# A cross-network tower on one core: a third PSUM buffer for VectorE's groups, and the turned rows in the gram product's buffer

## The chip, the cores and the metric

The kernel runs on one core of one Trainium2 chip. The metric is the device time of one execution in microseconds (us). Engines are TensorE (PE, with its weight loads shown as PEld), VectorE (DVE), ScalarE (ACT), GpSimd (POOL) and SyncE (SP, which issues DMAs).

## The reference

512 samples look up 39 rows of 16 numbers. Three cross layers follow, each of them all products of the samples' features with the layer's input, multiplied by a filter; then a small multilayer network:

```
e = stack([tbl_f[ids[:, f]] for f in range(39)], axis=1)      # 512 x 39 x 16
x0 = xk = e
for W in (f0, f1, f2):
    z = einsum('bfd,bgd->bfgd', x0, xk).reshape(b, f * g, d)
    cur = einsum('bpd,pm->bmd', z, W)                         # b x 128 x 16
    outs.append(cur); xk = cur
z = sum(concatenate(outs, axis=1), axis=-1)                   # 512 x 384
h = relu(concatenate([z, dense_ctx], axis=1) @ W_top1 + b_top1)
h = relu(h @ W_top2 + b_top2)
y = h @ W_top3
```

All of it is float32.

## The kernel before

The batch is cut into 16 blocks of 32 samples (512 columns of sample and depth), a block into 4 tiles of 128 columns. For layer 1 a tile's columns are the stationary operand: TensorE multiplies them by the whole filter in 10 **groups** of up to 512 outputs, which are 4 of the 39 features each. Written (t, g) below is group g of tile t. Each group is three matmuls, of high and low parts (lines 752, 753, 756), into one PSUM buffer of 512 float32, a whole bank. `PATTERN` gives groups 0, 2, 3, 5, 7, 8 of a tile to ScalarE ("a", three buffers psa in a ring) and groups 1, 4, 6, 9 to VectorE ("d", two buffers psd in a ring). ScalarE scales each 128 outputs by a feature value (`x0c`, line 607) into `parts`; VectorE adds its scaled groups onto what ScalarE has left there (line 503), so the n-th d group of a tile waits for the n-th a group too. When all ten are in, VectorE reduces them to `cur1` (line 485, `finish_tile`). `parts` and `cur1` exist twice, for even and odd tiles.

TensorE may start a group when its buffer is free: `act_prods` counts ScalarE's finished groups, `acc_steps` VectorE's. In between, at fixed places of its stream, TensorE does the next block's layer 0 (`layer0`, 7 steps k of pair products; k = 0, 1, 6 as plain float32 at line 713, the others as three split matmuls), turns the next block's feature rows so that they are per-partition scalars (`turn_x0`, line 721, after (1, 5), into `pst`), and after the last group of a tile makes the gram product of the tile before (`grams`, line 730, into `psg`, two passes of 320 columns). ScalarE copies the turned rows to `x0c` (`scalars`), the grams to `gram` (`gram_out`), layer 0's result to `x1h` (`high_part`) and the high parts of pair products to `z0h` (`pair_high_part`).

GpSimd makes the pair products (`z0`, line 341) and low parts `z0l` (line 348), spreads `x0c` for the gram product (`spread`, line 357), and fetches embeddings three blocks ahead, one index column and gather per feature quartet (`row_numbers`, line 329, and `gather`). `row_numbers` for column c waits until VectorE has done 6 + c of the block's 16 d groups. All queues are in program order; the order is written by hand in tables such as `ZH_AT` and `SCALARS_AT`. Blocks 1 to 13 are one hardware loop on TensorE, VectorE and ScalarE, and blocks 1 to 12 on GpSimd; gathers end with block 12.

After block 15 comes layer 2, by the grams (39 steps of three matmuls), and the network on top, whose first layer takes `ps0`, `pst`, `psa0`, `psa1` as its buffers.

Of the kernel before, what the change touches and what calls it, by code (L numbers as in the profile page):

```python
# [25 lines left out]
F32 = mybir.dt.float32  # L26
# [3 lines left out]
ACT = mybir.ActivationFunctionType  # L30
AX = mybir.AxisListType

B, F, D = 512, 39, 16
M = 128
BB = 32
NBLK = B // BB
COLS = BB * D
TILES = 4
TB = BB // TILES
# [3 lines left out]
ROWS = SPT * F  # L43
# [4 lines left out]
FX = F + 1  # L48


PATTERN = ["adaadadaad", "adaadadaad", "adaadadaad", "adaadadaad"]
D_RING, A_RING = 2, 3
D_OFF = [sum(p.count("d") for p in PATTERN[:t]) for t in range(TILES + 1)]
A_OFF = [sum(p.count("a") for p in PATTERN[:t]) for t in range(TILES + 1)]
ND, NA = D_OFF[TILES], A_OFF[TILES]
SLOTS = max(p.count("a") for p in PATTERN)
assert ND % D_RING == 0 and NA % A_RING == 0
assert all(p.count("a") == SLOTS and p.count("d") <= SLOTS for p in PATTERN)


# [15 lines left out]
HIGH_AT_FIRST = {(3, 2): 0, (3, 3): 1, (3, 5): 2}  # L76
LOW_AT = {(2, 2): 0, (2, 3): 1, (3, 0): 2}
LOW_AT_FIRST = {(3, 1): 0, (3, 2): 1, (3, 3): 2}
SCALARS_AT = {(2, 3): 0, (2, 5): 1, (3, 2): 2}
PIECES = [(0, 2), (2, 4), (4, L0T)]  # L80
FIRST_PIECES = [(0, 1), (1, 3), (3, 5), (5, L0T)]
GATHERS_FROM = 6
# [21 lines left out]
def starts(b):  # L104

    return isinstance(b, int) and b == 0


def build(nc, tables, ids, w0a, w0b, w1, w2, wt1, bt1, wt2, bt2, wt3, dense, mask, ident, out):
    scratch = nc.dram_tensor("x0_rows", (F + SHIFTS, BB, D), F32, kind="Internal").ap()  # L110
    scr_rows = scratch.rearrange("f b d -> f (b d)")
    H1T, H2T = wt1.shape[1] // 128, wt2.shape[1] // 128

    with ExitStack() as ctx:
# [70 lines left out]
                return w2early[:, M * a:M * b]  # L185
            return w2late[:, M * (a - W2_EARLY):M * (b - W2_EARLY)]

        psd = [ctx.enter_context(nc.psum_tensor(f"psd{i}", [128, 512], F32)) for i in range(D_RING)]
        psa = [ctx.enter_context(nc.psum_tensor(f"psa{i}", [128, 512], F32)) for i in range(A_RING)]
        ps0 = ctx.enter_context(nc.psum_tensor("ps0", [128, 512], F32))  # L190
        pst = ctx.enter_context(nc.psum_tensor("pst", [128, 512], F32))
        psg = ctx.enter_context(nc.psum_tensor("psg", [128, 512], F32))

        ids_in, w0_in, w1_in, const_in, mlp_in, wt2_in, w2a_in, w2b_in = (
            sem(n) for n in ("ids_in", "w0_in", "w1_in", "const_in", "mlp_in", "wt2_in", "w2a_in", "w2b_in"))
# [22 lines left out]
        y_d = sem("y_d")  # L218
# [237 lines left out]
        def _(dve):  # L456
# [32 lines left out]
            def block_of(b, ahead, at=None):  # L489
                for t in range(TILES):  # L490
                    T = b * TILES + t
                    groups = [g for g in range(NG) if PATTERN[t][g] == "d"]
                    for n, g in enumerate(groups):
                        d = D_OFF[t] + n
                        y = psd[d % D_RING]
                        if n == 0:
                            dve.wait_ge(x0c_ready, T + 1)

                        dve.wait_ge(act_prods, b * NA + A_OFF[t] + n + 1)
                        dve.wait_ge(y_d, b * ND + d + 1)  # L500
                        for j in range(min(GF, F - GF * g)):
                            acc = lanes(parts[:, t % 2, n, :], j)
                            op = dve.scalar_tensor_tensor(acc, y[:, M * j:M * j + M],  # L503
                                                          x0c[:, t, GF * g + j:GF * g + j + 1], acc,
                                                          ALU.mult, ALU.add)
                        op.then_inc(acc_steps, 1)
                        if (t, n) == (0, 0):
                            low_part(b, TILES - 1)
                        if ahead:
                            if (t, n) == (SUM_AT_FIRST if starts(b) else SUM_AT):  # L510
                                sum_cur0(b + 1, at)
                            low_at = LOW_AT_FIRST if starts(b) else LOW_AT
                            if (t, n) in low_at:
                                low_part(b + 1, low_at[t, n])
                    finish_tile(b, t)
# [41 lines left out]
        def _(act):  # L557
# [23 lines left out]
            def scalars(b, t):  # L581
                act.wait_ge(tr_done, b + 1)
                if not starts(b):
                    act.wait_ge(acc_steps, (b - 1) * ND + D_OFF[t + 1])
                    act.wait_ge(x0d_ready, (b - 1) * TILES + t + 1)
                act.activation(x0c[:, t, 0:F], pst[:, ROWS * t:ROWS * t + F], ACT.Copy).then_inc(x0c_ready, 1)

            def gram_out(T, at):
                act.wait_ge(g2_done, T + 1)
# [3 lines left out]
            def block_of(b, ahead):  # L593
                for t in range(TILES):
                    T = b * TILES + t
                    groups = [g for g in range(NG) if PATTERN[t][g] == "a"]
                    for n, g in enumerate(groups):
                        a = A_OFF[t] + n
                        y = psa[a % A_RING]
                        act.wait_ge(y_a, b * NA + a + 1)  # L600
                        if n == 0:
                            act.wait_ge(x0c_ready, T + 1)
                            if t >= 2 or not starts(b):
                                act.wait_ge(c1_ready, T - 1)
                        dst = parts[:, t % 2, n, :]
                        for j in range(GF):
                            op = act.activation(lanes(dst, j), y[:, M * j:M * j + M], ACT.Copy,  # L607
                                                scale=x0c[:, t, GF * g + j:GF * g + j + 1])
                        op.then_inc(act_prods, 1)
                        if n == 1 and (t >= 2 or not starts(b)):  # L610
                            at = (slice((T - 2) * TB, (T - 1) * TB) if isinstance(T, int)
                                  else bass.ds((T - 2) * TB, TB))
                            gram_out(T - 2, at)
                        zh_at = ZH_AT_FIRST if starts(b) else ZH_AT
                        if ahead and (t, n) in zh_at:
                            pair_high_part(b + 1, zh_at[t, n])
                        if t == 0 and n == 0:
                            high_part(b, 3)
                        if t == 0 and n == 2:
                            scalars(b, 3)  # L620
                        if ahead:
                            high_at = HIGH_AT_FIRST if starts(b) else HIGH_AT
                            if (t, n) in high_at:
                                high_part(b + 1, high_at[t, n])
                            if (t, n) in SCALARS_AT:
                                scalars(b + 1, SCALARS_AT[t, n])

            act.dma_start(ident_sb[0:ROWS, :], ident).then_inc(const_in, 16)
            act.dma_start(mask_sb[:, :], mask).then_inc(const_in, 16)
# [49 lines left out]
            act.activation(s2[:, :], psg[:, :], ACT.Copy).then_inc(s2_ready, 1)  # L679
            act.wait_ge(const_in, 16 * 5)  # L680
            act.wait_ge(c1_ready, NBLK * TILES)
            for m, y in enumerate([ps0, pst, psa[0], psa[1]][:H1T]):
                act.wait_ge(h1_done, m + 1)
                act.activation(h1[:, m, :], y[:, :], ACT.Relu, bias=bt1_sb[:, m:m + 1]).then_inc(h1_ready, 1)
            for m in range(H2T):
# [6 lines left out]
        def _(pe):  # L692
# [22 lines left out]
            def turn_x0(b):  # L715

                pe.wait_ge(loaded, 16 * (FIRST_DMAS + LOAD_DMAS * b))
                if not starts(b):
                    pe.wait_ge(x0c_ready, b * TILES)
                for t in range(TILES):  # L720
                    op = pe.transpose(pst[:, ROWS * t:ROWS * t + ROWS], x0t[0:ROWS, 128 * t:128 * t + 128], ident_sb[0:ROWS, :])
                op.then_inc(tr_done, 1)

            def grams(T, t):
# [8 lines left out]
            def block_of(b, ahead):  # L733
                for t in range(TILES):
# [4 lines left out]
                    for g in range(NG):  # L739
                        n = M * min(GF, F - GF * g)  # L740
                        c = slice(GF * M * g, GF * M * g + n)
                        if PATTERN[t][g] == "d":
                            y, full = psd[d % D_RING], y_d
                            if d >= D_RING or not starts(b):
                                pe.wait_ge(acc_steps, b * ND + d - D_RING + 1)
                            d += 1
                        else:
                            y, full = psa[a % A_RING], y_a
                            if a >= A_RING or not starts(b):
                                pe.wait_ge(act_prods, b * NA + a - A_RING + 1)  # L750
                            a += 1
# [5 lines left out]
                        if ahead:  # L757
# [3 lines left out]
                            if t == 1 and g == 5:  # L761
                                turn_x0(b + 1)
                        if g == NG - 1 and (t or not starts(b)):
                            grams(T - 1, (t - 1) % TILES)


# [19 lines left out]
            pe.wait_ge(mlp_in, 16 * 3)  # L786
            pe.wait_ge(s0_summed, NBLK)
            pe.wait_ge(x0c_ready, NBLK * TILES)
            banks = [ps0, pst, psa[0], psa[1]][:H1T]
            for m, y in enumerate(banks):  # L790
                c = slice(128 * m, 128 * m + 128)
                if m == 2:
                    grams(NBLK * TILES - 1, TILES - 1)
                    pe.wait_ge(act_prods, NBLK * NA)
                pe.matmul(y[:, :], wt1_sb[:, 0, c], s0[:, :], start=True, stop=False)
                pe.matmul(y[:, :], wt1_sb[0:16, 3, c], dense_sb, start=False, stop=False)  # L796
# [92 lines left out]
```

## Time and profile before

| | us |
|---|---|
| three executions | 724.42, 726.49, 2229.46; median 726.49 |
| the profiled execution | 722.3 |
| its span | 720.5 |
| PE busy | 647.5 (90%) |
| DVE busy | 537.1 (75%) |
| ACT busy | 524.1 (73%) |
| POOL busy | 451.6 (63%) |

The span is what the instructions of the trace cover; the profiled execution has 1.8 us around it. Busy is time with an instruction at work, so 90% for TensorE holds matmuls that overlap in the pipeline. Blocks 2 to 8 each last 38.6 us, from one (0, 0) to the next; block 7, from 315.12 to 353.75 us, is the one that is read here, and the end of block 6 before it.

### The profile page before, as it was taken

Reading aid. Unit: us, or ns where it says so; the run is one execution under the profiler, and the core shown is the slowest. Engines: PE = TensorE matmul, PEld = TensorE weight load, DVE = VectorE, ACT = ScalarE, POOL = GpSimd, SP = SyncE. Lnnn points to the kernel's source line nnn. Section 1 sums busy time; section 2 is a strip of 40 time slices with the busy share of each in tenths; the row PEclk is TensorE's granted clock in tenths of the full one; section 3 lists DMA queues with packets and bytes.
Section 4 is the critical chain, followed back from the end, with each engine's and each line's share of the span. In section 5 each row is a group of like instructions: output and inputs, shape, how many; then the busy total and the mean of one; then the engine's idle time right before and its main releaser. Section 6 shows DMA issues by size and latency. Waiting matters only on the chain. (4 is left out here: it accounts for less than half of the span.)

```text
span 720.5 us, 11962 instructions
## 1 busy us (share of the span) xinstructions
PE 647.5 (90%) x2571; PEld 473.9 (66%) x2571; DVE 537.1 (75%) x1152; ACT 524.1 (73%) x1846; POOL 451.6 (63%) x537
## 2 busy tenths in 40 slices
PE   0789899999999898989899999979898999989988
PEld 0257677676767676767677676757676777765663
DVE  1556769697878787887969697867879696988880
ACT  2157678787888787777788787857777787887762
POOL 6857976868595868686776859485867635101330
PEclk9989999999999999999999999999999999999999
DMA  7551321222222130413022222203130230301000
GB/s 200 119 115 55 60 64 44 61 52 61 52 40 74 36 78 10 97 15 88 18 63 49 60 52 60 53 10 101 11 89 18 64 91 0 106 1 40 30 1 0
DMA packets 58221, 40.29 MB, mean 56 GB/s; under 512 B 36625, under 2 KB 41055, under 8 KB 58202
## 3 DMA queue, kind: packets, MB, share of 16 engines
q1 hardware_dynamic: 52376, 38.73, 21.7%
q0 software_dynamic: 5120, 1.29, 2.1%
q10 hardware_dynamic: 706, 0.06, 0.1%
q8 instruction: 6, 0.10, 0.1%
q14 instruction: 13, 0.11, 0.0%
HBM read 38.13 MB, written 1.94 MB: 56 GB/s over the span
## 5 line engine op out<-in xcount | busy, mean ns | idle before, releaser
L607 ACT ACTIVATE parts<-psa,x0c 128x128 f32<-128x128 f32 x1536 | 440.6, 409 | 101.4 <-PE psa L756 101.1
L503 DVE SCALAR_TENSOR_TENSOR parts<-psd,x0c,parts 128x128 f32<-128x128 f32 x960 | 266.6, 343 | 107.7 <-PE psd L756 65.2
L485 DVE TENSOR_REDUCE cur<-parts 128x128 f32<-128x3072 f32 x64 | 214.6, 3353 | 25.1 <-ACT parts L607 16.7
L752 PE MATMUL psa<-w1h,x1h 128*128 128x512 f32 x384 | 177.4, 462 | 11.8 <-ACT parts L607 9.6
L333 POOL DMA_INDIRECT emb<-tables,idx x140 | 135.5, 968 | 45.3 <-POOL idx L329 25.0
L756 PE MATMUL psa<-w1h,x1l 128*128 128x512 f32 x384 | 152.8, 398 | 0.0
L753 PE MATMUL psa<-w1l,x1h 128*128 128x512 f32 x384 | 152.8, 398 | 0.0
L341 POOL TENSOR_TENSOR pairs<-x0t,pairs 117x512 f32<-117x512 f32 (+1 forms) x105 | 133.8, 1292 | 7.8 <-DMA pairs<-x_rows 7.0
L752 PE MATMUL psd<-w1h,x1h 128*128 128x512 f32 (+1 forms) x256 | 104.9, 410 | 32.7 <-DVE parts L503 32.5
L752 PEld LDWEIGHTS psa<-w1h,x1h 128*128 128x128 f32 x384 | 72.8, 190 | 46.7 <-ACT parts L607 20.8
L756 PE MATMUL psd<-w1h,x1l 128*128 128x512 f32 (+1 forms) x256 | 98.0, 383 | 0.0
L753 PE MATMUL psd<-w1l,x1h 128*128 128x512 f32 (+1 forms) x256 | 97.9, 382 | 0.0
L348 POOL TENSOR_TENSOR z0l<-pairs,z0h 117x512 fp32r<-117x512 f32 x60 | 77.3, 1288 | 21.5 <-ACT z0h L564 21.3
L752 PEld LDWEIGHTS psd<-w1h,x1h 128*128 128x128 f32 x256 | 48.5, 190 | 62.0 <-DVE parts L503 53.2
L753 PEld LDWEIGHTS psa<-w1l,x1h 128*128 128x128 f32 x384 | 73.2, 191 | 22.5 <-issue 4.4
L756 PEld LDWEIGHTS psa<-w1h,x1l 128*128 128x128 f32 x384 | 72.9, 190 | 18.0
L357 POOL TENSOR_TENSOR x0d<-x0c,mask_sb 128x320 f32<-128x320 f32 x64 | 46.4, 724 | 54.5 <-PE psg L730 54.0
L329 POOL TENSOR_TENSOR idx<-ids_sb 128x1 int32<-128x1 int32 x130 | 25.0, 192 | 80.9 <-DVE parts L503 79.9
L564 ACT ACTIVATE z0h<-pairs 117x512 fp32r<-117x512 f32 x60 | 41.3, 689 | 35.2 <-POOL pairs L341 35.2
L713 PE MATMUL ps<-pairs,w0s 117*128 117x512 f32 (+1 forms) x104 | 55.8, 627 | 0.0
L753 PEld LDWEIGHTS psd<-w1l,x1h 128*128 128x128 f32 x256 | 48.7, 190 | 9.2 <-issue 0.2
L756 PEld LDWEIGHTS psd<-w1h,x1l 128*128 128x128 f32 x256 | 48.5, 190 | 8.9
(82 smaller groups left out, 537.6 us busy)
## 6 DMA issues: line engine op xcount, KB each, us to landing
pairs<-x_rows SPq DMA_DIRECT2D x113, 156.0 KB
pairs<-x_rows SPq DMA_DIRECT2D x30, 234.0 KB
x0t<-x_rows SPq DMA_DIRECT2D x16, 234.0 KB
emb<-tables,idx POOLq DMA_INDIRECT x140
x_rows<-emb SPq DMA_DIRECT2D x14, 72.0 KB
wt_sb<-w_top SPq DMA_DIRECT2D x1, 768.0 KB, 7.3
parts<-w SPq DMA_DIRECT2D x1, 704.0 KB, 4.7
x_rows<-emb SPq DMA_DIRECT2D x14, 40.0 KB
```

Of the source, the lines that this page charges most:

```text
L333: pool.indirect_dma_start(emb[0:n, c, :], None, tables, bass.IndirectOffsetOnAxis(idx[0:n, c:c + 1], 0)).then_inc(gathered, 16)
L341: pool.tensor_tensor(pairs[0:rows, k, :], x0t[0:rows, :], pairs[0:rows, k, :], ALU.mult).then_inc(z0_ready, 1)
L348: pool.tensor_tensor(z0l[0:ROWS, c], pairs[0:ROWS, k, :], z0h[0:ROWS, c].bitcast(F32), ALU.subtract).then_inc(z0l_ready, 1)
L357: pool.tensor_tensor(x0d[:, t % 2, :, :], x0c[:, t, :].unsqueeze(1).to_broadcast([128, TB, FX]), mask_sb[:, :].unsqueeze(2).to_broadcast([ ...
L485: dve.tensor_reduce(cur1[:, t % 2, :], parts[:, t % 2, :, :].rearrange("p k (j m i) -> p m (k j) i", m=M, i=2), AX.XY, ALU.add).then_inc(c ...
L503: op = dve.scalar_tensor_tensor(acc, y[:, M * j:M * j + M], x0c[:, t, GF * g + j:GF * g + j + 1], acc, ALU.mult, ALU.add)
L564: act.activation(z0h[0:ROWS, c], pairs[0:ROWS, k, :], ACT.Copy).then_inc(z0h_ready, 1)
L607: op = act.activation(lanes(dst, j), y[:, M * j:M * j + M], ACT.Copy, scale=x0c[:, t, GF * g + j:GF * g + j + 1])
L713: pe.matmul(ps0[:, :], w0s[0:rows, k, :], pairs[0:rows, k, :], start=(k == 0), stop=(k == L0_END)).then_inc(l0_steps, 1)
L752: pe.matmul(y[:, 0:n], hi, w1h[:, c], start=True, stop=False)
L753: pe.matmul(y[:, 0:n], hi, w1l[:, c], start=False, stop=False)
L756: pe.matmul(y[:, 0:n], lo, w1h[:, c], start=False, stop=True).then_inc(full, 1)
```

## The change

There are now three psd buffers. The 16 d groups of a block take them in turn, 0, 1, 2, 0, ..., but the last takes buffer 1, since 16 isn't a multiple of 3; `D_SINCE` tells for each group how many groups ago its buffer was last used (2 for groups (0, 4) and (3, 9), otherwise 3 or 4), and TensorE waits for `acc_steps` accordingly. The eighth bank comes from `pst`: the turned rows go into columns 320 to 475 of `psg`, whose first 320 hold the gram product. Before, a turn was four transposes that gave three copies of the 39 features (117 columns); now it is four plain float32 matmuls with the first 39 columns of the identity, so one copy. Since one bank now has two writers and two kinds of reader, waits and places change: `turn_x0` waits until the gram products so far have been copied; `grams` waits for the copies to `x0c` that stand before it; `scalars` stands after ScalarE's second group of a tile, for x0c tile 3 in tile 0 (before: after the third), tile 0 in tile 2 (before: after the fourth), and tiles 1 and 2 both in tile 3 (before: after the last group of tile 2, and after the third group of tile 3). The network's second buffer is psd2 in place of pst, with a wait for VectorE's last group.

```diff
-D_RING, A_RING = 2, 3
+A_RING = 3
+D_BANKS = 3
+D_BANK = [d % D_BANKS for d in range(ND - 1)] + [1]
+D_SINCE = [next(n for n in range(1, ND) if D_BANK[(d - n) % ND] == D_BANK[d]) for d in range(ND)]
-SCALARS_AT = {(2, 3): 0, (2, 5): 1, (3, 2): 2}
+SCALARS_AT = {2: [0], 3: [1, 2]}
...
-        pst = ctx.enter_context(nc.psum_tensor("pst", [128, 512], F32))
         psg = ctx.enter_context(nc.psum_tensor("psg", [128, 512], F32))
+        pst = psg[:, TB * FX:TB * FX + TILES * F]
...
             def scalars(b, t):
                 act.wait_ge(tr_done, b + 1)
                 if not starts(b):
                     act.wait_ge(acc_steps, (b - 1) * ND + D_OFF[t + 1])
+                    act.wait_ge(act_prods, (b - 1) * NA + A_OFF[t + 1])
                     act.wait_ge(x0d_ready, (b - 1) * TILES + t + 1)
-                act.activation(x0c[:, t, 0:F], pst[:, ROWS * t:ROWS * t + F], ACT.Copy)
+                act.activation(x0c[:, t, 0:F], pst[:, F * t:F * t + F], ACT.Copy)
...
-                        if t == 0 and n == 2:
+                        if n == 1 and t == 0:
                             scalars(b, 3)
+                        if n == 1 and ahead:
+                            for i in SCALARS_AT.get(t, []):
+                                scalars(b + 1, i)
...
             def turn_x0(b):
+                if not isinstance(b, int) or b > 1:
+                    pe.wait_ge(g2_copied, (b - 1) * TILES)
                 for t in range(TILES):
-                    op = pe.transpose(pst[:, ROWS * t:ROWS * t + ROWS], x0t[0:ROWS, 128 * t:128 * t + 128], ident_sb[0:ROWS, :])
+                    op = pe.matmul(pst[:, F * t:F * t + F], x0t[0:ROWS, 128 * t:128 * t + 128], ident_sb[0:ROWS, 0:F], start=True, stop=True)
...
                         if PATTERN[t][g] == "d":
-                            y, full = psd[d % D_RING], y_d
-                            if d >= D_RING or not starts(b):
-                                pe.wait_ge(acc_steps, b * ND + d - D_RING + 1)
+                            y, full = psd[D_BANK[d]], y_d
+                            if d >= D_SINCE[d] or not starts(b):
+                                pe.wait_ge(acc_steps, b * ND + d - D_SINCE[d] + 1)
...
                         if g == NG - 1 and (t or not starts(b)):
+                            if t == 0:
+                                pe.wait_ge(x0c_ready, b * TILES + 4)
+                            elif ahead and t in SCALARS_AT:
+                                pe.wait_ge(x0c_ready, (b + 1) * TILES + SCALARS_AT[t][-1] + 1)
                             grams(T - 1, (t - 1) % TILES)
```

TensorE in tile 1 of the loop, from the turned rows on; the numbers behind psd and psa are the buffers. Before:

```order
L721 MATMUL pst<-ident_sb,x0t 128x117 x3
L745 REGISTER_ALU
L752 MATMUL psd0<-w1h,x1h 128x512 [waits acc_steps]
L753 MATMUL psd0<-w1l,x1h 128x512
L756 MATMUL psd0<-w1h,x1l 128x512
```

Now:

```order
L725 ISA
L731 MATMUL psg<-ident_sb,x0t 128x39 [waits g2_copied,x0c_ready,loaded]
L731 MATMUL psg<-ident_sb,x0t 128x39 x3
L755 REGISTER_ALU
L762 MATMUL psd0<-w1h,x1h 128x512 [waits acc_steps]
L763 MATMUL psd0<-w1l,x1h 128x512
L766 MATMUL psd0<-w1h,x1l 128x512
```

The rows have 39 columns in place of 117, go to psg, and wait for one semaphore more; their place is the same.

ScalarE in tile 0 of the loop, from the gram copy after its second group to its third. Before:

```order
L590 ISA [waits g2_done]
L590 ACTIVATE gram<-psg 128x40x8
L561 ISA
L562 ISA [waits z0_ready]
L564 ACTIVATE z0h<-pairs 117x512 [waits l0_steps]
L600 REGISTER_ALU
L607 ACTIVATE parts<-psa,x0c 128x128 [waits y_a]
L607 ACTIVATE parts<-psa,x0c 128x128 x3
L585 ISA [waits acc_steps,tr_done]
L586 ACTIVATE x0c<-pst 128x39 [waits x0d_ready]
```

Now:

```order
L597 ISA [waits g2_done]
L597 ACTIVATE gram<-psg 128x40x8
L567 ISA
L568 ISA [waits z0_ready]
L570 ACTIVATE z0h<-pairs 117x512 [waits l0_steps]
L591 ISA [waits acc_steps,tr_done]
L592 ISA [waits act_prods]
L593 ACTIVATE x0c<-psg 128x39 [waits x0d_ready]
L607 REGISTER_ALU
L614 ACTIVATE parts<-psa,x0c 128x128 [waits y_a]
L614 ACTIVATE parts<-psa,x0c 128x128 x3
```

The copy to x0c has moved ahead of the third group, and stands behind the high part z0h that waits for GpSimd's pair product.

## Rows read from the trace of the kernel before

**Rows 1.** The page, TensorE's granted clock in 40 equal slices of the span.

```profile
PEclk9989999999999999999999999999999999999999
```

**Rows 2.** Waits of 120 to 580 us: us in total, times, longest.

```profile
ACT z0h L564 <- POOL pairs L341: 33.8, 12, 5.3
...
PE psd L752 <- DVE parts L503: 22.0, 23, 1.2
```

**Rows 3.** Timeline, PE, 312 to 354: start, duration, work, count, [idle <- releaser].

```profile
312.10 0.50 PE L752 MATMUL psd<-w1h,x1h 128*128 128x512 f32 x1 [1.19 <-DVE parts L503]
...
314.30 0.34 PE L752 MATMUL psd<-w1h,x1h 128*128 128x384 f32 x1
...
314.82 0.70 PE L730 MATMUL psg<-x0d,cur 128*128 128x320 f32 x2
...
315.12 0.64 PE L752 MATMUL psa<-w1h,x1h 128*128 128x512 f32 x1
...
320.46 0.50 PE L752 MATMUL psd<-w1h,x1h 128*128 128x512 f32 x1 [0.74 <-DVE parts L503]
...
323.39 0.50 PE L752 MATMUL psa<-w1h,x1h 128*128 128x512 f32 x1 [0.40 <-ACT parts L607]
...
325.87 0.64 PE L752 MATMUL psa<-w1h,x1h 128*128 128x512 f32 x1
...
353.75 0.64 PE L752 MATMUL psa<-w1h,x1h 128*128 128x512 f32 x1
```

**Rows 4.** Timeline, the other engines, 310 to 322.

```profile
310.93 1.12 DVE L503 SCALAR_TENSOR_TENSOR parts<-psd,x0c,parts 128x128 f32<-128x128 f32 x4
...
312.16 1.12 DVE L503 SCALAR_TENSOR_TENSOR parts<-psd,x0c,parts 128x128 f32<-128x128 f32 x4
...
312.22 0.19 POOL L329 TENSOR_TENSOR idx<-ids_sb 128x1 int32<-128x1 int32 x1 [2.17 <-DVE parts L503]
...
320.25 3.77 POOL L341 TENSOR_TENSOR pairs<-x0t,pairs 117x512 f32<-117x512 f32 x3
...
321.67 0.63 ACT L564 ACTIVATE z0h<-pairs 117x512 fp32r<-117x512 f32 x1 [2.54 <-POOL pairs L341]
```

**Rows 5.** Timeline, DVE at the end of tile 1.

```profile
336.50 0.87 DVE L503 SCALAR_TENSOR_TENSOR parts<-psd,x0c,parts 128x128 f32<-128x128 f32 x3 [1.65 <-PE psd L756]
```

**Rows 6.** Timeline, PE around the turned rows.

```profile
332.42 0.56 PE L721 MATMUL pst<-ident_sb,x0t 117*128 117x117 f32 x4
332.74 0.48 PE L752 MATMUL psd<-w1h,x1h 128*128 128x512 f32 x1
```

**Rows 7.** Weight loads by line: shapes, count, busy us, mean ns, idle before.

```profile
L753 PEld LDWEIGHTS psa<-w1l,x1h 128*128 128x128 f32 x384 | 73.2, 191 | 22.5 <-issue 4.4
...
L721 PEld LDWEIGHTS pst<-ident_sb,x0t 117*128 117x128 f32 x64 | 7.9, 145 | 5.7 <-issue 3.8
...
L838 PEld LDWEIGHTS psg<-parts,wt_sb 128*1 128x1 f32 x4 | 0.2, 81 | 1.5 <-ACT parts L687 1.5
```

**Rows 8.** Timeline, PE at two of its clock's falls, and after the second.

```profile
85.87 0.50 PE L752 MATMUL psa<-w1h,x1h 128*128 128x512 f32 x1 [1.45 <-ACT parts L607]
...
87.79 0.50 PE L752 MATMUL psd<-w1h,x1h 128*128 128x512 f32 x1 [0.95 <-DVE parts L503]
...
481.39 0.80 PE L752 MATMUL psa<-w1h,x1h 128*128 128x512 f32 x1 [3.18 <-ACT parts L607]
...
485.31 0.64 PE L752 MATMUL psa<-w1h,x1h 128*128 128x512 f32 x1
```

**Rows 9.** Windows: length, busy PE, PEld, DVE, ACT, POOL, granted clock, DMA.

```profile
88.56:91.97 3.41, 3.41 (x7) 1.98 (x6) 1.53 (x6) 3.24 (x12) 3.41 (x4) 0.50 0.28 33
481.10:484.50 3.40, 3.11 (x7) 2.45 (x8) 1.59 (x6) 3.40 (x14) 3.40 (x4) 0.50 0.15 15
```

**Rows 10.** Timeline, blocks 14 and 15: PE at (0, 8), DVE at a (t, 9).

```profile
597.72 0.80 PE L752 MATMUL psa<-w1h,x1h 128*128 128x512 f32 x1
...
645.49 0.87 DVE L503 SCALAR_TENSOR_TENSOR parts<-psd,x0c,parts 128x128 f32<-128x128 f32 x3 [0.80 <-PE psd L756]
```

More of the change, by code:

```diff
@@ L56 @@
 SLOTS = max(p.count("a") for p in PATTERN)
-assert ND % D_RING == 0 and NA % A_RING == 0
+assert NA % A_RING == 0
+D_BANKS = 3
+D_BANK = [d % D_BANKS for d in range(ND - 1)] + [1]
+D_SINCE = [next(n for n in range(1, ND) if D_BANK[(d - n) % ND] == D_BANK[d]) for d in range(ND)]
+assert min(D_SINCE) == 2
 assert all(p.count("a") == SLOTS and p.count("d") <= SLOTS for p in PATTERN)
@@ L186, in w2_part @@
             return w2late[:, M * (a - W2_EARLY):M * (b - W2_EARLY)]
-        psd = [ctx.enter_context(nc.psum_tensor(f"psd{i}", [128, 512], F32)) for i in range(D_RING)]
+        psd = [ctx.enter_context(nc.psum_tensor(f"psd{i}", [128, 512], F32)) for i in range(D_BANKS)]
         psa = [ctx.enter_context(nc.psum_tensor(f"psa{i}", [128, 512], F32)) for i in range(A_RING)]
         ps0 = ctx.enter_context(nc.psum_tensor("ps0", [128, 512], F32))
-        pst = ctx.enter_context(nc.psum_tensor("pst", [128, 512], F32))
         psg = ctx.enter_context(nc.psum_tensor("psg", [128, 512], F32))
+        pst = psg[:, TB * FX:TB * FX + TILES * F]
         ids_in, w0_in, w1_in, const_in, mlp_in, wt2_in, w2a_in, w2b_in = (
@@ L494, in block_of @@
                         d = D_OFF[t] + n
-                        y = psd[d % D_RING]
+                        y = psd[D_BANK[d]]
                         if n == 0:
@@ L584, in scalars @@
                     act.wait_ge(acc_steps, (b - 1) * ND + D_OFF[t + 1])
+                    act.wait_ge(act_prods, (b - 1) * NA + A_OFF[t + 1])
                     act.wait_ge(x0d_ready, (b - 1) * TILES + t + 1)
-                act.activation(x0c[:, t, 0:F], pst[:, ROWS * t:ROWS * t + F], ACT.Copy).then_inc(x0c_ready, 1)
+                act.activation(x0c[:, t, 0:F], pst[:, F * t:F * t + F], ACT.Copy).then_inc(x0c_ready, 1)
             def gram_out(T, at):
@@ L624, in block_of @@
                                 high_part(b + 1, high_at[t, n])
-                            if (t, n) in SCALARS_AT:
-                                scalars(b + 1, SCALARS_AT[t, n])
             act.dma_start(ident_sb[0:ROWS, :], ident).then_inc(const_in, 16)
@@ L681, in _ @@
             act.wait_ge(c1_ready, NBLK * TILES)
-            for m, y in enumerate([ps0, pst, psa[0], psa[1]][:H1T]):
+            for m, y in enumerate([ps0, psd[2], psa[0], psa[1]][:H1T]):
                 act.wait_ge(h1_done, m + 1)
@@ L788, in _ @@
             pe.wait_ge(x0c_ready, NBLK * TILES)
-            banks = [ps0, pst, psa[0], psa[1]][:H1T]
+            banks = [ps0, psd[2], psa[0], psa[1]][:H1T]
             for m, y in enumerate(banks):
                 c = slice(128 * m, 128 * m + 128)
+                if m == 1:
+                    pe.wait_ge(acc_steps, NBLK * ND)
                 if m == 2:
```

## The prediction

> **What bounds the kernel now.** I read the page first: 16 blocks, TensorE busy nine tenths of the time, its granted clock near 1.0 but for short dips [rows 1]. So either its own work or the little waits in it must be the bound. The list of waits between 120 and 580 us, which is 12 blocks, shows two of interest [rows 2]: TensorE waits 22.0 us for VectorE to free a psd buffer, the very thing that a third buffer takes away, and ScalarE waits 33.8 us, about once a block, for GpSimd's pair product.
>
> The timeline shows where these lie in a block of 38.63 us, 315.12 to 353.75 [rows 3]. TensorE waits at (3, 6) for 1.19 us and at (0, 6) for 0.74 us, both for psd, and at (0, 8) for 0.40 us, for ScalarE. Before asking what they cost, one asks what the wait at (0, 8) hangs on. Group (0, 8) needs ScalarE's third group of the tile out of its buffer; that stands in ScalarE's queue behind z0h, which started only at 321.67, after 2.54 us of waiting for GpSimd's product [rows 4]. GpSimd made it as the first of three products from 320.25 on, and had been at work without a pause since 312.22 (four gathers, two index columns, two products and then this one); what started that stretch was an index column that waited for VectorE's group (3, 1), done at 310.93 + 1.12 = 312.05 [rows 4]. VectorE does (3, 1) straight after the reduction of tile 2, not when TensorE pleases. And from (0, 8) on, tile 1 goes at TensorE's pace: VectorE's last group there had waited 1.65 us for its matmuls [rows 5].
>
> So the block is a ring: VectorE (3, 1) at 312.05, GpSimd, ScalarE's z0h at 321.67, its third group, TensorE (0, 8) at 323.39, tile 1, the reductions of tiles 1 and 2, VectorE (3, 1) again. The psd waits at (3, 6) and (0, 6) both lie between VectorE (3, 1) and (0, 8), beside the 9.4 us of GpSimd, and not on the ring. While GpSimd gathers, they cost nothing.
>
> **The change, part by part.**
>
> *Third buffer, blocks 2 to 13.* The wait at (3, 6) goes. Group (3, 9) must take buffer 1, last used by (3, 4), which VectorE finishes at 312.16 + 1.12 = 313.28 [rows 4]; so it starts at about 313.33 in place of 314.30 [rows 3], and the next block 0.97 us earlier. At (0, 6) another 0.74 us goes. What is late next is (0, 8): GpSimd, z0h and the third group are where they were, so its wait grows to 0.97 + 0.74 + 0.40 = 2.1 us, somewhat more by the slower first matmul after each wait that goes. Worth: 0 us, since the cover is GpSimd's stretch; if that cover were gone, the two would be worth 1.7 us a block.
>
> *The turned rows.* They lie after (1, 5) in tile 1, where nothing hides TensorE's time, so each ns counts once for each of 15 blocks. Before, four transposes took 0.32 us from first start to the next group's start, and that group lasts 0.08 longer than a plain 0.40: 0.40 us, 0.10 each [rows 6]. A plain float32 product is two passes, as the gram pair shows [rows 3], so there are eight passes, each with its own weight load. No row has such short passes with full loads. Lower bound: at the transposes' pace, 8 x 0.10 = 0.80, +0.40 us a block. Upper bound: the whole load of 0.191 [rows 7] and then the stream, 39 of 320 columns of a gram pass. That pass takes 0.27 us (0.30 from the pair at 314.82 to the group at 315.12, and 0.24 more that this group lasts, for two [rows 3]), so 0.03: 8 x 0.22 = 1.78, +1.38. I take the load without what a load of a single column also takes, 0.191 - 0.081 = 0.110 [rows 7], plus 0.03, or 0.14 a pass, since the same rule gives the transposes 0.145 - 0.081 + about 0.04 = 0.10, as measured. So 8 x 0.14 - 0.40 = +0.72 us, x 15 = **+10.8 us** (+6.0 to +20.7). By the Trainium skill ("TensorE: Matmul & The Clock Gate", Terms) the transpose mode is four times faster for float32. Counting columns alone by it, 39 columns would weigh like 156 against 117 before, that is 0.40 x 4/3, +0.13 us a block and 2 us in all, and the sum below would be about 731; it leaves out the loads, and no row here shows it.
>
> *TensorE's clock.* At (0, 8) three short waits become one of 2.1 us or more. The clock fell from 2.4 to 1.2 GHz twice after the first block [rows 9]: at 88.56, after waits of 1.45 and 0.95 us that came together, and at 481.1, during one of 3.18 us [rows 8]. It did not fall in the other blocks, with 0.74 + 0.40 us in the same place. The new wait is nearest to 1.45 + 0.95. I take it that the clock falls in 9 of the 11 blocks from 2 to 13 where it had not (block 11 has its fall already). A fall costs what block 11 shows from (0, 8) to the first group of tile 1: 485.31 - 481.39 = 3.92 us [rows 8] against 325.87 - 323.39 = 2.48 [rows 3], so 1.44 us, on the ring because tile 1 goes at TensorE's pace. **+13.0 us** (0 to +15.8).
>
> *The end.* GpSimd stops gathering with block 12. In block 14, (0, 8) starts without a wait [rows 10], so there the psd waits do count: 0.97 at its start, 0.74 at its (0, 6), and again 0.97 at its end, 2.7 us. In block 15 nothing is prepared for a next block, and VectorE has a gap of 0.80 us before each (t, 9), because TensorE was held at (t, 6); there are four such rows [rows 10]. With three buffers it is never idle there: 4 x 0.80 = 3.2 us. Together **-5.9 us** (-2 to -7).
>
> *Waits and places that cost nothing.* The copy to x0c stands before ScalarE's third group in tile 0 and no longer between fourth and third in tile 2: some 0.1 us is put on the ring and as much taken off. The turn waits for the copy of the last gram, done near the second group of tile 1, over 1 us before TensorE is at (1, 5); behind it would be all of TensorE. The waits before the gram product are for copies that ScalarE makes seven groups earlier. The network's wait for VectorE's last group ends before that buffer is reached. SP's and GpSimd's queues are not reordered.
>
> *Sum.* 722.3 + 10.8 + 13.0 - 5.9 = 740.2, against the profiled execution's own time. The two undisturbed runs shown are 2.1 and 4.2 us above that one (their median row is 726.49), so I add 2: **742 us**, +2.2% on 726.49.
>
> **Rivals.**
>
> 1. *The clock holds.* Nothing else differs: 722.3 + 10.8 - 5.9 + 2 = 729 us; with the lower bound of the turned rows 724. For it: the wait of 2.1 us is shorter than both that went with a fall, in all. Against: it comes at once, in ten blocks and more. The Trainium skill ("TensorE: Matmul & The Clock Gate", A second HAM failure mode: psum-queue depth-cycling) holds frequent short idles between groups to be what makes the clock swing. By that rule before would be the worse kernel, and the clock would hold now. The trace shows three short waits a block and a clock of 1.0 but for the dips, so I don't follow it.
>
> 2. *The other side: the psd waits are on the path.* If GpSimd's stretch can start or end sooner than I think, the ring closes through VectorE and psd, and each of 12 blocks loses 1.19 + 0.74 = 1.9 us, or all 22.0 of [rows 2]; with no long wait the clock holds: 722.3 + 10.8 - 22.0 - 5.9 + 2 = 707 us. It decides from GpSimd finishing its product more than about 2 us sooner after VectorE (3, 1). Against it speaks that GpSimd's stretch has no pause.
>
> 3. *The turned rows cost their upper bound*, a full load each, with falls of the clock: 742 + 9.9 = 752 us.
>
> **How the numbers follow.** A measurement of this kernel tells 2%, some 14.5 us, from no change, so the line is at 741. Chances: forecast 0.50, which by the turned rows' bounds goes from 737 to 748 and lies on both sides of the line; rival 1, 0.30; rival 2, 0.10; rival 3, 0.10. The range holds the forecast and rival 1 nearly whole and most of rival 3: 725 to 752; rival 2 is left out. Slower by over 2%: 0.33 of the 0.50, and 0.10, so 0.43. Faster by over 2%: 0.09, from rival 2. Within: 0.48.
>
> **What would show it.** In the changed profile: in blocks 2 to 13 ScalarE's wait for GpSimd's pair product grows from 2.5 to 3.5 us; waits for psd at (3, 6) and (0, 6) gone, one of 0.4 us or more left at (3, 9); TensorE's wait at (0, 8) 2 us or more; granted clock of 0.50 after it in most blocks, and a block of 39.3 us without a fall, 40.8 with one. From the first turned row to the next group 1.1 us. In block 15 reductions 7.6 us apart, not 8.4. I am wrong if blocks without a fall are shorter than 38.6 us: then the ring isn't the bound.

## The result

The changed kernel takes **737.25 us** (median of 4 runs, 735.67 to 740.33) against 726.06 for the kernel before: a ratio of 1.0163 with a 95% interval of 1.0123 to 1.0202. It is slower, by clearly more than nothing, and whether by 2% the interval leaves open. The forecast was 742 us in 725 to 752. The profiled execution took 738.17 us with a span of 736.3, against 722.3 and 720.5 before.

### The profile after

The page, busy time and granted clock over the 40 slices:

```profile
span 736.3 us, 12208 instructions
...
PE 661.8 (90%) x2635; PEld 493.2 (67%) x2635; DVE 534.8 (73%) x1152; ACT 522.9 (71%) x1846; POOL 450.1 (61%) x537
...
PEclk9899999999999999999999999998999999999999
...
PE 44%; issue 15%; POOL 13%; ACT 12%; DVE 4%; ACTq 1%; DVEq 1%; POOLq 1%
```

Nothing here names a cause. Slices of 18 us average a short fall of the clock nearly away. So go to the list of waits (waiting instruction <- releaser: us in all, how often, the longest), again from 120 to 580 us:

```profile
POOL idx L335 <- DVE parts L509: 77.5, 44, 2.1
...
ACT z0h L570 <- POOL pairs L347: 43.8, 12, 6.1
...
PE psa L762 <- ACT parts L614: 29.0, 11, 5.1
...
PE psd L762 <- DVE parts L509: 5.7, 12, 0.5
```

In the kernel before, TensorE's wait for ScalarE in the same window was:

```profile
PE psa L752 <- ACT parts L607: 8.2, 12, 3.2
```

Set against [rows 2], TensorE's waits for psd went from 22.0 us to 5.7, as the third buffer promises. ScalarE's wait for GpSimd grew by 10.0 us over 12 blocks, and TensorE's wait for ScalarE grew from 8.2 us to 29.0, in which block 13's is not counted, since it ends at 580.34. The time was not won, it was moved to one place. The timeline of block 9 (start, duration, and in brackets the idle time before, with what ended it) shows that place:

```profile
401.21 1.12 DVE L509 SCALAR_TENSOR_TENSOR parts<-psd,x0c,parts 128x128 f32<-128x128 f32 x4
...
402.50 0.19 POOL L335 TENSOR_TENSOR idx<-ids_sb 128x1 int32<-128x1 int32 x1 [2.05 <-DVE parts L509]
...
403.61 0.44 PE L762 MATMUL psd<-w1h,x1h 128*128 128x384 f32 x1 [0.48 <-DVE parts L509]
...
404.53 0.64 PE L762 MATMUL psa<-w1h,x1h 128*128 128x512 f32 x1
...
412.27 0.63 ACT L570 ACTIVATE z0h<-pairs 117x512 fp32r<-117x512 f32 x1 [3.74 <-POOL pairs L347]
...
414.08 0.77 PE L762 MATMUL psa<-w1h,x1h 128*128 128x512 f32 x1 [2.69 <-ACT parts L614]
...
418.16 0.64 PE L762 MATMUL psa<-w1h,x1h 128*128 128x512 f32 x1
```

These are the rows that answer to [rows 3] and [rows 4]. (3, 9) still waits, 0.48 us, at 403.61. The block begins at 404.53, and (0, 6) has no wait any more. VectorE's (3, 1) is done at 402.33, GpSimd starts at 402.50 and the z0h that follows starts 9.8 us later, as in block 9 before (389.48 to 399.29, 9.8); in block 7 it is 9.4 us (322.80 to 332.20) against 9.5 before. (0, 8) is at 414.08 after 2.69 us of waiting, and the first group of tile 1 comes 4.08 us behind it, against 2.48. In the windows from about (0, 8) to that group (length, busy time of PE, PEld, DVE, ACT and POOL with counts, granted clock, DMA share, GB/s), block 7 and block 9:

```profile
333.90:337.00 3.10, 2.98 (x12) 2.17 (x13) 2.00 (x7) 3.10 (x13) 3.10 (x4) 1.00 0.14 14
414.14:417.55 3.41, 3.41 (x8) 2.60 (x9) 1.97 (x7) 3.41 (x14) 3.41 (x4) 0.50 0.12 12
```

A granted clock of 0.50 is the 1.2 GHz level. Such a fall stands behind (0, 8) in 11 of the 12 blocks from 2 to 13, where before only block 11 had one [rows 8, 9]. Block 7 is the one without:

```profile
334.02 0.50 PE L762 MATMUL psa<-w1h,x1h 128*128 128x512 f32 x1 [2.32 <-ACT parts L614]
...
336.50 0.64 PE L762 MATMUL psa<-w1h,x1h 128*128 128x512 f32 x1
...
343.04 0.98 PE L731 MATMUL psg<-ident_sb,x0t 117*128 117x39 f32 x8
...
343.85 0.48 PE L762 MATMUL psd<-w1h,x1h 128*128 128x512 f32 x1
...
363.88 0.63 PE L762 MATMUL psa<-w1h,x1h 128*128 128x512 f32 x1
```

**Where 15.9 us went.** Blocks are counted from the start of their first group. Up to block 2 the changed kernel is 0.75 us ahead (121.28 against 122.03). Blocks 2 to 13 take 490.60 us against 468.39, +22.2. Block 14 takes 36.48 against 37.93, −1.45, and from block 15 to the end it is 87.99 against 92.14, −4.15. That makes +15.9, the difference of the spans before they are rounded. Inside the 22.2: block 7, with no fall, takes 39.05 us (324.84 to 363.88) against 38.63 in [rows 3], +0.42; most of the others take 40.71, so a fall is worth 1.66. Ten new falls are 16.6 and twelve times 0.42 is 5.0, together 21.6 of 22.2. The rest is block 11, which has its fall in both kernels and is 1.06 us longer, not 0.42 (43.91 against 42.85).

In block 15 the reductions of VectorE stand 7.31 to 7.34 us apart, with nothing between them but its groups [rows 10 has the gap of before]:

```profile
657.18 3.35 DVE L491 TENSOR_REDUCE cur<-parts 128x128 f32<-128x3072 f32 x1
660.45 3.96 DVE L509 SCALAR_TENSOR_TENSOR parts<-psd,x0c,parts 128x128 f32<-128x128 f32 x15
664.50 3.35 DVE L491 TENSOR_REDUCE cur<-parts 128x128 f32<-128x3072 f32 x1
```

### The profile page after: what moved, and what is told of

Read it like the earlier page. It is cut to its first block, busy times and chain, and to the rows that moved or that the text cites. A ratio compares the mean times of both kernels' runs of the same rounds, so it can differ in the third digit from the quotient of the medians.

```text
span 736.3 us, 12208 instructions
## 1 busy us (share of the span) xinstructions
PE 661.8 (90%) x2635; PEld 493.2 (67%) x2635; DVE 534.8 (73%) x1152; ACT 522.9 (71%) x1846; POOL 450.1 (61%) x537
## 4 chain that ended last, share of the span: by engine, by line
PE 44%; issue 15%; POOL 13%; ACT 12%; DVE 4%; ACTq 1%; DVEq 1%; POOLq 1%
ACT parts L614 12%; POOL pairs L347 7%; PE psa L762 5%; PE psa L766 5%; PE psa L763 5%; PE ps L721 5%; POOL emb L339 4%; DVE parts L509 3%; PE psd L762 3%; PE psg L740 3%; PE psd L766 3%; PE psd L763 3%; PE ps L716 2%; PE ps L718 2%; PE ps L717 2%
## 5 line engine op out<-in xcount | busy, mean ns | idle before, releaser
L614 ACT ACTIVATE parts<-psa,x0c 128x128 f32<-128x128 f32 x1536 | 432.3, 417 | 109.9 <-PE psa L766 93.0
L491 DVE TENSOR_REDUCE cur<-parts 128x128 f32<-128x3072 f32 x64 | 214.6, 3352 | 20.2 <-ACT parts L614 10.8
L762 PE MATMUL psa<-w1h,x1h 128*128 128x512 f32 x384 | 178.3, 464 | 38.8 <-ACT parts L614 37.4
L762 PE MATMUL psd<-w1h,x1h 128*128 128x512 f32 (+1 forms) x256 | 102.4, 400 | 6.8 <-DVE parts L509 6.6
L721 PE MATMUL ps<-pairs,w0s 117*128 117x512 f32 (+1 forms) x104 | 63.4, 706 | 0.0
```

What stands on the lines that cost most here:

```text
L491: dve.tensor_reduce(cur1[:, t % 2, :], parts[:, t % 2, :, :].rearrange("p k (j m i) -> p m (k j) i", m=M, i=2), AX.XY, ALU.add).then_inc(c ...
L721: pe.matmul(ps0[:, :], w0s[0:rows, k, :], pairs[0:rows, k, :], start=(k == 0), stop=(k == L0_END)).then_inc(l0_steps, 1)
L762: pe.matmul(y[:, 0:n], hi, w1h[:, c], start=True, stop=False)
```

## The experiments

Ten kernels in three sets. The kernel before, run with each set, had medians of 722.63, 724.56 and 718.82 us; each ratio is against the runs of its own set.

**The third buffer and the product apart.** First, the changed kernel with two buffers again:

```diff
-D_BANK = [d % D_BANKS for d in range(ND - 1)] + [1]
+D_BANK = [d % 2 for d in range(ND)]
```

> The changed kernel, its d groups on two psd buffers in turn as before; the turned rows, psg and all waits stay as changed. Theory (the ring goes through GpSimd, the third buffer only gathers three waits into one, and the long wait makes the clock fall): the waits at (3, 6) and (0, 6) are back, (0, 8) waits well under 1 us, no falls of the clock in blocks 2 to 13 but where GpSimd is late, a block of 39.05 us (as the changed kernel's one block without a fall), and the gain at the end is lost: 722.3 + 0.42 x 15 = 728.6 profiled, 730 to 732 timed, that is faster than the changed kernel's 737. Rival (the product in place of the transposes, or the new waits, cost all of it themselves): 737 or more, since a buffer is taken away on top.

Measured: 729.89 us, ratio 1.0100 (1.0067 to 1.0132). Of the blocks 2 to 13 nine take 39.1 us, and the clock falls in block 11 alone. Its waits from 120 to 580 us:

```profile
ACT z0h L570 <- POOL pairs L347: 33.7, 12, 5.3
...
PE psd L762 <- DVE parts L509: 21.7, 24, 1.1
...
PE psa L762 <- ACT parts L614: 9.2, 12, 3.3
```

The first two are those of [rows 2] again, to 0.3 us, and the third was 8.2. The third buffer made the kernel 0.6% slower as the two ratios stand (1.0163 and 1.0100), or 7.4 us between the two medians, which come from different sets. The two intervals overlap, so the times alone leave this open; the traces carry it. Blocks 2 to 13 take 475.2 us with two buffers (125.00 to 600.16) and 490.6 with three. Without a fall a block is as long either way, 39.1 and 39.05: the third buffer is worth nothing there, and the falls come with it.

Then the kernel before with its four transposes made products, and nothing else:

```diff
-op = pe.transpose(pst[:, ROWS * t:ROWS * t + ROWS], x0t[0:ROWS, 128 * t:128 * t + 128], ident_sb[0:ROWS, :])
+op = pe.matmul(pst[:, ROWS * t:ROWS * t + F], x0t[0:ROWS, 128 * t:128 * t + 128], ident_sb[0:ROWS, 0:F], start=True, stop=True)
```

> The kernel before, where only the four transposes are replaced by four plain float32 products of 39 columns, in pst as before. Theory: the changed kernel's rows give 0.88 us from (1, 5)'s step to (1, 6) in place of 0.40, so 0.48 x 15 = 7.2 us on the ring, no falls: 723 + 7 = 730, ratio 1.010. Rival (the cost of 0.42 us a block without a fall comes from the x0c copies and the new waits): ratio 1.000.

Measured: 730.24 us, ratio 1.0086 (1.0054 to 1.0118), blocks of 39.10, +0.48 each, psd waits of 23.2 us. The product alone is as slow as the whole change without its third buffer, whose interval its own overlaps, and whose blocks are as long. Behind (0, 8) the clock never falls in its blocks 2 to 13. That settles the split: about 1% is the product, and what is over that comes with the third buffer.

The changed kernel with short turned rows (row 0 by a product, so that the whole tile of weights is as before; the others as transposes of the one copy):

```diff
-op = pe.matmul(pst[:, F * t:F * t + F], x0t[0:ROWS, 128 * t:128 * t + 128], ident_sb[0:ROWS, 0:F], start=True, stop=True)
+if t == 0:
+    pe.matmul(pst[:, 0:F], x0t[0:ROWS, 0:128], ident_sb[0:ROWS, 0:F], start=True, stop=True)
+else:
+    op = pe.transpose(pst[:, F * t:F * t + F], x0t[0:F, 128 * t:128 * t + 128], ident_sb[0:F, 0:F])
```

> The changed kernel, with three of the four turned rows as transposes of 39 rows and 39 columns in place of products. Theory: from the first turned row to the next group about 0.45 us in place of 0.9, so 0.4 to 0.5 us a block off the ring, 15 times, 6 to 7 us; the falls of the clock stay in most blocks: 729 to 732. Rival (the turned rows aren't on the path, and the 0.42 us a block come from the new place of the x0c copies): within 2 us of 737.

Measured: 730.67 us, ratio 1.0115 (1.0076 to 1.0153). The turn in its timeline:

```profile
340.03 0.31 PE L732 MATMUL psg<-ident_sb,x0t 117*128 117x39 f32 x2
...
340.28 0.38 PE L734 MATMUL psg<-ident_sb,x0t 39*128 39x39 f32 x3
...
340.58 0.50 PE L765 MATMUL psd<-w1h,x1h 128*128 128x512 f32 x1
```

It takes 0.55 us to the next group's start, against 0.81 (343.04 to 343.85) in the changed kernel. Blocks take 38.8 us without a fall and 40.4 with one. A block without a fall is 0.24 us shorter than the changed kernel's, where 0.4 to 0.5 was expected. That is 3.6 us over 15 blocks; the rest of the 6.6 us between the two medians (737.25 and 730.67) fits two falls fewer, so the expected time was met in part by luck. The falls are still there in nine blocks, and the product alone had none: they come with the long wait, not with the product.

**Is it the idle time that makes the clock fall?** Eight matmuls whose result nobody reads, put in blocks 1 to 13 into the wait before (0, 8):

```diff
+if (t, g) == (0, 7) and not isinstance(b, int):
+    pe.wait_ge(acc_steps, b * ND + 1)
+    for _ in range(FILLERS):
+        pe.matmul(psd[D_BANK[3]][:, :], hi, w1h[:, 0:512], start=True, stop=True)
```

> The changed kernel, with eight extra matmuls of 512 columns in blocks 1 to 13 between (0, 7) with its layer-0 step and (0, 8), into the psd buffer that (0, 9) overwrites; their result is not used. 8 x 0.233 = 1.87 us of work in a wait of about 2.6. Theory: TensorE has less idle time there, the clock doesn't fall, the ring keeps its length: the changed kernel's 11 falls of 1.66 us go, 737 - 18 = 719, faster than the kernel before (725). Rival (the falls are a by-product, the blocks are long for another reason): 737, or more by the added work.

Measured: 721.34 us, ratio 0.9991 (0.9960 to 1.0022), 2 us more than expected. The page's clock line, then the place in a block by the timeline, then two blocks in one window:

```profile
PEclk9899999999999999999999999999999999999999
```

```profile
283.37 2.42 PE L775 MATMUL psd<-w1h,x1h 128*128 128x512 f32 x8
...
286.29 0.50 PE L763 MATMUL psa<-w1h,x1h 128*128 128x512 f32 x1 [0.49 <-ACT parts L615]
...
288.77 0.64 PE L763 MATMUL psa<-w1h,x1h 128*128 128x512 f32 x1
```

```profile
316.00:394.00 78.00, 76.05 (x325) 58.85 (x324) 61.19 (x138) 60.40 (x225) 56.02 (x70) 1.00 0.24 52
```

TensorE does more, and the kernel is 1.7% shorter than the changed one, as the ratios stand. There is no fall left after the start; from (0, 8) to tile 1 it is 2.48 us again, and blocks take 39.1. The ring is as long as in the changed kernel's block without a fall, but with work in most of the wait the clock holds in every block. That shows idle time at that place to be needed for the falls. It also shows the rest: 39.1 a block is still no shorter than before, since GpSimd's stretch is untouched.

**What the third buffer is worth if the ring is cut.** Column c of GpSimd's indices waits for fewer of VectorE's groups, 2 + c in place of 6 + c, so that no gather is left for the stretch behind (3, 1). First in the changed kernel, then in the kernel before:

```diff
-GATHERS_FROM = 6
+GATHERS_FROM = 2
```

> The changed kernel, GATHERS_FROM 2 in place of 6: each index column waits for four d groups fewer, so GpSimd's stretch starts up to 4.7 us earlier. Theory (the ring goes through GpSimd's stretch): ScalarE's wait for the pair product and TensorE's wait at (0, 8) go, and blocks 2 to 13 come near the 36.5 us of block 14, in place of 40.7: 12 x 4.2 = 50 us less, 685 to 692. Rival (the ring closes elsewhere, or GpSimd's earlier work collides with VectorE or the DMAs): above 720.

> The kernel before (two psd buffers, transposes), with GATHERS_FROM 2 in place of 6 alone. Theory: with GpSimd off the ring, the psd waits at (3, 6) and (0, 6) are the bound again; blocks 2 to 13 come to block 14's 37.9 us in place of 38.6, and the two late blocks lose their excess (4.2 and 0.8): 12 x 0.7 + 5 = 13 us less, 708 to 711. Then the third buffer, worth nothing with late gathers, is worth some 18 us with early ones (690 against 709). Rival (the early gathers alone brought the changed kernel's 47 us, the buffer nothing): about 690.

Measured: **690.34 us**, ratio 0.9539 (0.9500 to 0.9578), and 710.97 us, ratio 0.9772 (0.9698 to 0.9847). In the changed kernel with early gathers z0h starts without a wait, right behind ScalarE's copies, and TensorE's one wait that is left in 120 to 580 us is psd at (3, 9); in the kernel before the old psd waits stay. The first kernel by its timeline, its waits and a window of 220 us, and then the waits of the second:

```profile
309.57 0.66 ACT L570 ACTIVATE z0h<-pairs 117x512 fp32r<-117x512 f32 x1
```

```profile
PE psd L762 <- DVE parts L509: 9.2, 13, 0.9
```

```profile
280.00:500.00 220.00, 215.19 (x916) 166.16 (x914) 182.84 (x414) 180.45 (x668) 167.93 (x209) 1.00 0.23 54
```

```profile
PE psd L752 <- DVE parts L503: 24.5, 25, 1.2
```

The same change that costs 1.6% with late gathers gains 2.4% with early ones, by the ratios (0.9539 against 0.9772), or 20.6 us between the medians of the two sets (710.97 − 690.34). The turned rows' price is paid in it too. With the short turned rows of the last experiment, which ran in one set with the kernel before's early gathers, it is 21.7 us (710.97 − 689.28). This is rival 2 of the prediction, reached by another edit: once GpSimd's stretch is off the ring, the ring closes through psd.

The opposite, a longer stretch in the kernel before (`GATHERS_FROM = 7`):

> The kernel before, GATHERS_FROM 7 in place of 6 alone: each index column waits for one d group more, so GpSimd's stretch starts with VectorE's (3, 4), done 1.2 us after its (3, 1). Theory (GpSimd's stretch is on the ring, TensorE's psd waits are not): blocks 2 to 13 get 1.2 us longer, the psd waits stay as they are and the wait at (0, 8) grows from 0.4 to 1.6 us; 12 x 1.2 = 14 us, ratio 1.020, more if the clock falls in some blocks. Rival (GpSimd has slack, and the psd waits make the block): ratio 1.000.

Measured: 745.29 us, ratio 1.0369 (1.0325 to 1.0412). A block takes 40.60, +1.98, where +1.2 was expected. From its timeline and its waits:

```profile
318.82 1.12 DVE L503 SCALAR_TENSOR_TENSOR parts<-psd,x0c,parts 128x128 f32<-128x128 f32 x4
...
320.12 0.19 POOL L329 TENSOR_TENSOR idx<-ids_sb 128x1 int32<-128x1 int32 x1 [2.52 <-DVE parts L503]
...
320.78 0.96 POOL L333 DMA_INDIRECT emb<-tables,idx  x1 [0.47 <-POOL idx L329]
...
321.76 0.73 POOL L357 TENSOR_TENSOR x0d<-x0c,mask_sb 128x320 f32<-128x320 f32 x1
```

```profile
PE psa L752 <- ACT parts L607: 28.2, 11, 4.5
...
PE psd L752 <- DVE parts L503: 22.1, 23, 1.2
```

Index column 6, in place of column 7, now is the one that waits for VectorE (3, 1), so the gather and the spread that follow it in GpSimd's queue stand behind (3, 1) as well, which I had not counted. From this index column to z0h it is now 11.40 us (320.12 to 331.52) against 9.45 before: 1.95 more, and the block is 1.98 longer. GpSimd's stretch is on the path, us by us. The psd waits are 22.1 us as before. That alone doesn't tell that they are off the path, since waits on it would stay as well; that taking them away left block 7 of the changed kernel no shorter does.

**Is the wait left at (3, 9) worth anything?** The table of psd buffers rotated by eight groups takes it away. In the changed kernel with nothing else:

```diff
+D_BANK = [D_BANK[(d + 8) % ND] for d in range(ND)]
```

> The changed kernel, its table of psd buffers turned by eight groups as in the version with early gathers; gathers and turned rows as changed. The wait at (3, 9), 0.64 us in each block, goes. Theory: with late gathers it lies beside GpSimd's stretch, so (0, 8) waits 0.64 us longer and the block stays 40.7 us with a fall of the clock, 39.05 without: 736 to 739. Rival (this wait is on the path): 12 x 0.64 = 8 us less, 729.

Measured: 738.66 us, ratio 1.0276 (1.0235 to 1.0317), span 736.6 against 736.3. The ratio is 1.1% above the changed kernel's 1.0163, because the kernel before took 718.82 us in this set and 726.06 in the other; so the blocks have to decide. Blocks 2 to 13 take 491.1 us against 490.6, 11 of them with a fall, as in the changed kernel. Its waits:

```profile
PE psa L763 <- ACT parts L615: 32.9, 12, 5.2
...
PE ps L722 <- DVE x1l L478: 4.5, 12, 0.4
```

The psd wait is gone whole (5.7 us in the changed kernel, 0.47 a block, where 0.64 was assumed). The 4.5 us for VectorE's x1l are new, 0.37 a block, at the product of layer 0 just before (0, 8). At (0, 8) 12 waits now make 32.9 us; in the changed kernel the twelfth lies outside the window, and all 12 make 31.3, so 1.6 us more. One more wait beside GpSimd's stretch, removed for nothing.

Last, the versions with early gathers taken on: with the short turned rows of above, and with those and the rotation.

> The changed kernel with early gathers (GATHERS_FROM 2) and three of four turned rows as transposes of 39 rows. Theory: the turn is on TensorE's path in this kernel too; it took 6.6 us off with late gathers, so 690 - 6.6 = 684, if part of it doesn't go into the wait at (3, 9); 683 to 688. Rival (the ring now closes through VectorE and ScalarE, and TensorE has slack): 690.

> As x6, and the table of psd buffers turned by eight groups, so that the two groups whose buffer was used two groups before are (1, 9) and (2, 4), not (3, 9) and (0, 4). In the changed kernel with early gathers (3, 9) starts 0.65 to 1.07 us late. Theory: VectorE has caught up in tile 1 (it waits for TensorE there), so the wait goes and nothing takes its place: up to 0.9 x 12 = 10 us less than x6, 674 to 682. Rival (VectorE's own work sets the block: 31 to 32 us of work and the gaps that its order forces): the wait moves, same as x6 within 2 us.

Measured: 689.28 us, ratio 0.9501 (0.9427 to 0.9576), and 686.23 us, ratio 0.9452 (0.9372 to 0.9532). The first is within the noise of early gathers alone and misses the 683 to 688 that were expected: blocks 2 to 13 take 442.5 us against 443.1, and psd waits went from 9.2 to 10.7 us, so most of what the turn saved came back at (3, 9). The second has the lowest median of this study, but missed what was expected of it by 4 us or more. The wait of each that was left, first without and then with the rotation:

```profile
PE psd L765 <- DVE parts L509: 10.7, 13, 0.9
```

```profile
PE ps L722 <- DVE x1l L478: 8.9, 13, 0.8
```

The wait for VectorE only changed its name, from psd to x1l: VectorE is late there whichever buffer asks. In the second kernel it is busy 384.5 of 460 us in the window of 120 to 580, and TensorE 451.0. What else bounds these two kernels no run settles.

## Why the prediction was right

**The ring, and the third buffer's worth of 0.** Right. The stretch from (3, 1) to z0h kept its length, and block 7 is 0.42 us longer than before, not shorter. ScalarE's wait for the product is 3.35 to 3.74 us (6.15 in block 11), with 3.5 foreseen; the waits at (3, 6) and (0, 6) are gone; (3, 9) waits 0.48, with 0.4 or more foreseen. The late gathers, early gathers and rotated table show it from three sides.

**The wait at (0, 8) and the clock.** Right in kind, a little small in size. The wait is 2.3 to 2.7 us (5.10 in block 11), with 2.1 or somewhat more foreseen. Falls: 10 new ones, with 9 foreseen (a number that was chosen, not worked out), at 1.66 us, with 1.44. The term is 16.6 in place of 13.0. The price was taken from block 11 of before, whose 3.40 us at the lower clock held 0.29 us of idle TensorE (3.11 busy, [rows 9]); in block 9 all 3.41 us are work, and half of them are lost. That the filler brings the clock and the time back is what carries the cause, not the fit of the sum.

**The turned rows.** Right in place, too dear. A block is longer by 0.42 to 0.48 (changed kernel, product alone) and not by 0.72. Eight passes take 0.89 us from the first start to the next group's, with the 0.08 that this group lasts longer: 0.11 each, with 0.14 foreseen. That is the size of the first term in my sum, the 0.110 of the load, without the 0.03 of stream that I had added. Whether the stream runs beside the next load is not shown. The rule was weaker than I made it look: it was checked on the transposes with a stream of "about 0.04", which no row gives. By the gram pass that I used for the product it would be 117/320 x 0.27 = 0.10, so 0.16 a transpose, where 0.10 was measured. So the rule does not give the transposes' time. What the runs show is 0.10 to 0.11 us for each of these short passes, with 39 columns or 117. So the term was 15 x 0.45 = 6.8, not 10.8.

**The end.** Block 14 is 1.45 shorter with a turn of 0.45 in it, and block 15 to the end 4.2: −6.1, with −5.9 foreseen. That the start is ahead by 0.75 us, with the turns of two of the 15 blocks in it, was not foreseen: some −1.6. No cause is shown for it: block 2 begins anywhere from 117.65 to 125.00 us in the profiled executions of the twelve kernels, and the clock falls in different places before it. Reductions in block 15 are 7.31 to 7.34 apart, with 7.6 foreseen and 8.4 before.

The sum by the profiled executions was 17.9 and is 15.9. Two sizes, turned rows too dear by 4.0 and falls too cheap by 3.6, nearly cancel; that is luck, and the forecast is better than its terms. Of the 4.75 us by which 742 was above 737.25, 2.0 are the sum (740.2 against 738.17), 1.8 what I added for the median, and 0.9 that this profiled execution lay above its median, not below. Two slips change nothing in this: 742 on 726.49 is +2.1%, not +2.2%, and with the upper bound of the turned rows the forecast reaches 752, not 748.

**The rivals.** Rival 1, the clock holds, failed as 11 of 12 blocks fell; the filler shows the kernel that it spoke of, at 721.3 us on a chip where before takes 722.6. By the Trainium skill ("TensorE: Matmul & The Clock Gate", A second HAM failure mode: psum-queue depth-cycling) frequent short idles between groups made the clock swing in another kernel. Here it was the other way: with short waits of 1.19, 0.74 and 0.40 us in a block [rows 3] the clock held, and with one of 0.47 and one of 2.3 to 2.7 it fell in 10 of 11 blocks. Rival 2 needed early gathers. Rival 3's full loads do not occur.

## What to carry to other kernels

A wait that takes much time in the list is not yet on the path. Follow what the next wait behind it hangs on; if that chain doesn't pass through the removed wait, the time turns up there whole. Three short waits merged into one can be worse than the three, since TensorE's clock may fall with it: look at the granted clock in windows of a few us at that place. And a buffer that pays nothing today can pay 2.4% after the real bound is moved, so try the two edits together: here one constant, with the buffer that had looked useless, gave 690 us where the kernel before took 723.

## What was not expected of the hardware

- Short float32 products of 39 columns go at 0.11 us a pass, and three transposes with 39 columns of weights at 0.10 (0.30 us from 340.28 to 340.58).
- What picks the blocks that fall is open; the length of the wait alone does not. Block 7 of the changed kernel waited 2.32 us and the clock did not fall. In block 11 it fell around a wait of 3.18 us in the kernel before, and held around 3.17 us with the product alone and around 3.30 us behind the fillers. In the kernel before with late gathers waits of 2.37 us at the same place had mostly no fall (3 of 12 blocks have one), though in these (0, 6) still waits and divides the idle time.
